# Narrow transposed scores, squares in PSUM, and 2 KB and 16 KB runs for the parts of queries and keys

## The reference

```python
qkv = x @ qkv_w + qkv_b; q, k, v = split(qkv)       # 16 heads of 16
# local attention, blocks of 128 queries; keys from 127 before the block to its end
dist = q_pos - k_pos; allowed = (dist > 0) & (dist <= 128) & (k_pos >= 0)
attn = softmax(where(allowed, q @ k.T / 4, -1e9)); local = attn @ v
# remote attention: each query against means of 8 tokens, 4 heads, chunks before its own
remote = softmax(masked(rq @ rk.T / 4)) @ rv @ rout_w + rout_b
gate = sigmoid(local @ gl_w + remote @ gr_w)
x = layernorm(x + (gate * local + (1 - gate) * remote) @ out_w + out_b)
# feed-forward with ternary weights, each product on its rms-normalized input
h = gelu(ternary(x / rms(x), w_up)); x = layernorm(x + ternary(h / rms(h), w_down))
```

## Time and profile before

| what | us |
|---|---|
| median of 3 runs (1351.72 to 1356.64) | 1356.45 |
| the profiled execution | 1356.7 |
| its span in the profile | 1354.9 |
| TensorE busy in the span | 1125.0 (83%) |
| VectorE busy | 1026.3 (76%) |
| GpSimd busy | 708.1 (52%) |
| ScalarE busy | 671.9 (50%) |

### The profile page before, as it was taken

How to read it: one execution, slowest core, us unless ns; L and a number is a source line. 1 busy time by engine, 2 the same in 40 slices (tenths; PEclk the granted TensorE clock), 3 DMA queues, 4 the chain that set the end, 5 groups by cost and what they waited for, 6 DMA issues and landing times.

```text
span 1354.9 us, 31716 instructions
## 1 busy us (share of the span) xinstructions
PE 1125.0 (83%) x12704; PEld 690.3 (51%) x12704; DVE 1026.3 (76%) x2048; ACT 671.9 (50%) x1024; POOL 708.1 (52%) x866
## 2 busy tenths in 40 slices
PE   4667989897998989897987989798888989785855
PEld 2334545564655556464654555465555545454433
DVE  7755777878877787888787886888787687876566
ACT  2113455564646546464646555464655545462624
POOL 6413546473644636473654646374563647364643
PEclk9676989899988989899999999899898889997877
DMA  6984190846639192754729093663919275471000
GB/s 167 120 111 64 51 124 21 120 70 97 78 85 106 34 124 53 107 82 84 91 68 122 20 128 62 98 76 84 106 45 114 52 104 79 86 80 34 1 16 16
DMA packets 114482, 107.68 MB, mean 79 GB/s; under 512 B 13312, under 2 KB 113792, under 8 KB 114304
## 3 DMA queue, kind: packets, MB, share of 16 engines
q1 hardware_dynamic: 114336, 105.65, 52.2%
HBM read 71.55 MB, written 34.08 MB: 78 GB/s over the span
## 4 chain that ended last, share of the span: by engine, by line
PE 39%; DMA 21%; DVE 20%; SPq 6%; POOL 5%; issue 5%; ACT 3%; DVEq 0%; POOLq 0%
DMA Ks<-parts_scratch 18%; PE oacc L1372 7%; PE work L1321 7%; PE scores L1354 7%; SPq L446 3%; DMA parts_scratch<-parts 3%; DVE x L1035 3%; PE work L1382 3%; SPq L449 2%; DVE x L1043 2%; PE work L1444 2%; PE work L1203 2%; PE work L1326 2%; POOL parts L573 2%; DVE nmax L977 2%
## 5 line engine op out<-in xcount | busy, mean ns | idle before, releaser
L743 ACT ACTIVATE Pt<-scores 128x1024 f32<-128x1024 f32 (+1 forms) x256 | 231.8, 914 | 157.9 <-PE oacc L1372 94.6
L609 POOL TENSOR_TENSOR h_lo<-hbuf,h_hi 128x512 f16<-128x512 f32 x128 | 175.4, 1372 | 239.6 <-DVE h_hi L1088 239.6
L977 DVE TENSOR_REDUCE nmax<-work 128x3 f32<-128x480 f32 x352 | 217.5, 637 | 68.4 <-PE work L1326 64.1
L581 POOL TENSOR_SCALAR_AFFINE_SELECT Pt<-Pt 128x512 f32<-128x512 f32 x256 | 163.3, 638 | 130.4 <-ACT Pt L743 129.5
L1444 PE MATMUL work<-xnT,wup_t 128*128 128x512 f16 x512 | 151.6, 432 | 32.1 <-DVE xnT L1079 32.1
L1321 PE MATMUL work<-Ks,Qs 98*32 98x160 bf16 x4096 | 139.1, 243 | 39.1 <-DMA Ks<-parts_scratch 21.5
L1354 PE MATMUL scores<-Qs,Ks 100*128 100x256 bf16 (+1 forms) x1024 | 144.1, 267 | 3.1 <-ACT Pt L743 1.8
L1372 PE MATMUL oacc<-Pt,Vp 128*32 128x256 f32 (+1 forms) x2048 | 144.9, 360 | 1.9 <-POOL Pt L585 1.8
L1321 PEld LDWEIGHTS work<-Ks,Qs 98*32 98x32 bf16 x4096 | 77.2, 98 | 102.4 <-issue 40.9
L1093 DVE TENSOR_TENSOR oT<-oT,hsq 128x512 f32<-128x512 f32 x112 | 121.5, 1085 | 10.0 <-ACT hsq L784 10.0
L1228 PE MATMUL scores<-xT,wqk 128*128 128x512 f32 x256 | 116.3, 608 | 13.4 <-ACT xT L678 13.4
(11 more groups left out here) (166 smaller groups left out, 2082.0 us busy)
## 6 DMA issues: line engine op xcount, KB each, us to landing
parts_scratch<-parts SPq DMA_DIRECT2D x48, 512.0 KB, 3.0
Qs<-parts_scratch SPq DMA_DIRECT2D x96, 256.0 KB, 14.7
Ks<-parts_scratch SPq DMA_DIRECT2D x96, 256.0 KB, 16.5
xtok<-L_attn_x SPq DMA_DIRECT2D x16, 512.0 KB, 22.4
xres<-L_attn_x SPq DMA_DIRECT2D x16, 512.0 KB, 21.7
y<-ytok SPq DMA_DIRECT2D x16, 512.0 KB, 3.0
Qs<-L_ffn_w_up SPq DMA_DIRECT2D x1, 1024.0 KB, 7.0
Qs<-L_ffn_w_down SPq DMA_DIRECT2D x1, 1024.0 KB, 8.2
```

Source lines behind the costliest of these rows:

```text
L581: ins = pool.affine_select(out=pt[:, :, 0:P], in_=pt[:, :, 0:P], compare_op=ALU.is_gt, fill=0.0, base=0, pattern=[[0, 4], [1, P]], channel ...
L609: pool.tensor_tensor(h_lo[:, t % NR, :], hbuf[:, t % 2, :], h_hi[:, t % NR, :], ALU.subtract).then_inc(h_lo_ready, 1)
L743: nc.scalar.activation(Pt[:, u % NPT, :, 0:w], scores[:, slot, :, :].rearrange("p k (h q) -> p (k h) q", h=2)[:, :, 0:w], ACT.Exp, scale=S ...
L977: nc.vector.tensor_reduce(nmax[:, :, :].rearrange("p b h -> p (b h)")[:, first:first + n], work[:, slot, 0:n * BAND].rearrange("p (h c) -> ...
```

## The change

1. `scores_T` issues for each head and block of keys four matmuls of 32 keys each instead of one of 128; each moves only the queries that its keys can reach (up to 160), into its own 32 partitions of PSUM. Heads are placed in the stacks in another order (`place_of`).
2. The columns of `wqk` are permuted in the prologue (feature first, then head) by ScalarE from a raw copy that lies in `xres`; the bias is loaded to match in eight loads. With that, DRAM holds each part of queries or keys as 128 rows of 2 KB, and each stack row is one run of 16 KB. `Ks` has one padding of 128 columns in all.
3. `restack` writes the query parts as soon as two chunks are ready, waits, reads the six query stacks, then writes the key parts, waits and reads the six key stacks. The wait for the weighing of the sequence before stands ahead of it all.
4. The square is written over the Gelu's input in PSUM; VectorE adds from there, and the slot is free after the add. `hsq` stays only as room for the ternary weights.
5. GpSimd adds the output bias after the last mask, all four blocks in a row.

```diff
+STACKED = 16 * 2 * len(QPART)
+def place_of(h):
+    return h % (H // 2) * 2 + h // (H // 2)
...
-        Ks = [sb(f"Ks{k}", [P, H, P + S], BF16) for k in range(2)]
+        Ks = [sb(f"Ks{k}", [P, P + H * S], BF16) for k in range(2)]
...
-        parts_dram = nc.dram_tensor("parts_scratch", [3, 2 * D, S], BF16, kind="Internal").ap()
+        parts_dram = nc.dram_tensor("parts_scratch", [3, 2, P, 2 * S], BF16, kind="Internal").ap()
...
-            (wqk[:, :, :], qkv_w[:, 0:2 * D].rearrange("(t p) n -> p t n", p=P)),
+            (wqk_raw, qkv_w[:, 0:2 * D].rearrange("(t p) n -> p t n", p=P)),
...
-            (bqk[:, :], qkv_b[0:2 * D].rearrange("(t p) -> p t", p=P)),
...
+        loads += [(bqk[h:P:H // 2, :], qkv_b[0:2 * D].rearrange("(t h d) -> h d t", t=4, d=HD)[h])
+                  for h in range(H // 2)]
...
             def restack(s):
                 if not s.first:
-                    wait_alone(sp, stacks_in[1 - s.par], (s.half + s.par) * (16 * 2 * len(QPART)))
-                for j in range(3):
-                    wait_alone(sp, (part0, part1, part2)[j], count(s, 4, 3))
-                    sp.dma_start(parts_dram[j].rearrange("(t p) n -> p t n", p=P), parts[:, j, :, :]
-                                 ).then_inc(parts_out, 16)
+                    wait_alone(sp, stacks_in[1 - s.par], (s.half + s.par) * STACKED)
                 if s.known and s.i < 2:
                     wait_alone(sp, q_consts, s.i + 1)
                 else:
                     wait_alone(sp, pv_done, count(s, NU, -NU - 1))
-                wait_alone(sp, parts_out, count(s, 1, 0) * 48)
-                for r in range(len(QPART)):
-                    rows = slice(HD * r, HD * r + HD)
-                    sp.dma_start(Qs[s.par][rows, :, :],
-                                 parts_dram[QPART[r], 0:D].rearrange("(h d) n -> d h n", d=HD)
-                                 ).then_inc(stacks_in[s.par], 16)
-                    sp.dma_start(Ks[s.par][rows, :, P:P + S],
-                                 parts_dram[KPART[r], D:2 * D].rearrange("(h d) n -> d h n", d=HD)
-                                 ).then_inc(stacks_in[s.par], 16)
+                for k in range(2):
+                    for j in range(3):
+                        wait_alone(sp, (part0, part1, part2)[j], count(s, 4, 2 * k + 1))
+                        sp.dma_start(parts_dram[j, k], parts[:, j, 2 * k:2 * k + 2, :].rearrange("p t n -> p (t n)")
+                                     ).then_inc(parts_out, 16)
+                    wait_alone(sp, parts_out, count(s, 2, k) * 48)
+                    for r in range(len(QPART)):
+                        rows = slice(HD * r, HD * r + HD)
+                        stack = Qs[s.par][rows, :, :].rearrange("p h n -> p (h n)") if k == 0 else \
+                            Ks[s.par][rows, P:P + H * S]
+                        sp.dma_start(stack, parts_dram[(QPART, KPART)[k][r], k].rearrange(
+                            "(d h) n -> d (h n)", d=HD)).then_inc(stacks_in[s.par], 16)
...
                     mask(s, u)
...
-                    if u % NB == NB - 1:
-                        add_bias(s, u // NB)
+                for b in range(NB):
+                    add_bias(s, b)
...
+                    gelu = nc.scalar.activation(hbuf[:, t % 2, :], work[:, slot, :], ACT.Gelu)
+                    if t == 0:
+                        gelu.then_inc(w_taken[slot], 1)
+                        act.wait_ge(w_taken[slot], n + 1)
+                    else:
+                        gelu.then_inc(h_act, 1)
+                        act.wait_ge(h_act, count(s, FT - 1, t - 1))
-                    nc.scalar.activation(h_sum[:, :] if t == 0 else hsq[:, t % 2, :], hbuf[:, t % 2, :],
+                    nc.scalar.activation(h_sum[:, :] if t == 0 else work[:, slot, :], hbuf[:, t % 2, :],
                                          ACT.Square).then_inc(h_sq, 1)
...
+            for t in range(KT):
+                nc.scalar.activation(wqk[:, t, :].rearrange("p (c d h) -> p c d h", c=4, d=HD),
+                                     wqk_raw[:, t, :].rearrange("p (c h d) -> p c d h", c=4, d=HD),
+                                     ACT.Copy).then_inc(wqk_ready, 1)
...
-                        nc.vector.tensor_tensor(h_sum[:, :], h_sum[:, :], hsq[:, t % 2, :], ALU.add
-                                                ).then_inc(h_added, 1)
+                        nc.vector.tensor_tensor(h_sum[:, :], h_sum[:, :], work[:, slot, :], ALU.add
+                                                ).then_inc(w_taken[slot], 1)
...
                 for c in range(4):
-                    mm = nc.tensor.matmul(scores[:, slot, c // 2, (c % 2) * 2 * P:(c % 2) * 2 * P + w],
-                                          kk[0:KB, 4 * hg + c, P + j * P:2 * P + j * P],
-                                          q[0:KB, 4 * hg + c, j * P:j * P + w], start=True, stop=True)
+                    place = place_of(4 * hg + c)
+                    key = P + place * S + j * P
+                    for g in range(NG):
+                        lo, hi = g * GT, min(g * GT + BAND, w)
+                        mm = nc.tensor.matmul(
+                            scores[g * GT:(g + 1) * GT, slot, c // 2,
+                                   (c % 2) * 2 * P + lo:(c % 2) * 2 * P + hi],
+                            kk[0:KB, key + lo:key + lo + GT],
+                            q[0:KB, place, j * P + lo:j * P + hi], start=True, stop=True)
```

More of the change, by code:

```diff
@@ L287, in build @@
         ones_set = sem("ones_set")
+        wqk_ready = sem("wqk_ready")
         consts = sem("consts")
@@ L335, in build @@
         xn_hi = sem("xn_hi")
+        h_act = sem("h_act")
         h_sq = sem("h_sq")
@@ L357, in build, with in_blocks @@
         nat = nat_all[:, 0:FT * D], nat_all[:, FT * D:FT * D + KT * F]
-        ternary = [t[:, :, :].rearrange("p k n -> p (k n)").bitcast(BF16) for t in (hbuf, hsq)]
+        ternary = [t[:, :, :].rearrange("p k n -> p (k n)").bitcast(BF16) for t in (hbuf, tern_up)]
         below = Vp[:, 1, :, :].rearrange("p b n -> p (b n)").bitcast(BF16)[:, 0:FT * D]
+        wqk_raw = xres[:, :, :].rearrange("p b d -> p (b d)").rearrange("p (t n) -> p t n", t=KT)
         def in_pairs(stack):
-            return stack[:, :, :].bitcast(F32)
+            flat = stack[:, :, :].rearrange("p h n -> p (h n)") if len(stack.shape) == 3 else stack[:, :]
+            return flat.bitcast(F32)
+        def in_blocks(rows):
+            return rows.rearrange("p (b c) -> p b c", c=P)
         ONE_PAIR = float(np.array([0x3F803F80], np.uint32).view(np.float32)[0])
@@ L420, in load_xres @@
             def load_xres(s):
-                if not s.first:
+                if s.first:
+                    wait_alone(sp, wqk_ready, KT)
+                else:
                     for t in range(2):
@@ L571, in p_step @@
                     if t == 0 and not s.first:
-                        pool.wait_ge(parts_out, count(s, 1, -1) * 48)
+                        pool.wait_ge(parts_out, count(s, 2, -1) * 48)
                     pool.tensor_tensor(parts[:, 2, t, :], qk_rest[:, t % 2, :], parts[:, 1, t, :],
@@ L684, in p_step @@
                     if t == 0 and not s.first:
-                        act.wait_ge(parts_out, count(s, 1, -1) * 48)
+                        act.wait_ge(parts_out, count(s, 2, -1) * 48)
                     nc.scalar.activation(parts[:, 0, t, :], p_bank(bank), ACT.Identity,
@@ L778, in f_step @@
                         act.wait_ge(h_sq, count(s, FT, t - 2))
-                    nc.scalar.activation(hbuf[:, t % 2, :], work[:, slot, :], ACT.Gelu
-                                         ).then_inc(w_taken[slot], 1)
-                    act.wait_ge(w_taken[slot], n + 1)
-                    if t >= 3:
-                        act.wait_ge(h_added, count(s, FT - 1, t - 3))
-                    nc.scalar.activation(h_sum[:, :] if t == 0 else hsq[:, t % 2, :], hbuf[:, t % 2, :],
+                    gelu = nc.scalar.activation(hbuf[:, t % 2, :], work[:, slot, :], ACT.Gelu)
+                    if t == 0:
+                        gelu.then_inc(w_taken[slot], 1)
+                        act.wait_ge(w_taken[slot], n + 1)
+                    else:
+                        gelu.then_inc(h_act, 1)
+                        act.wait_ge(h_act, count(s, FT - 1, t - 1))
+                    nc.scalar.activation(h_sum[:, :] if t == 0 else work[:, slot, :], hbuf[:, t % 2, :],
                                          ACT.Square).then_inc(h_sq, 1)
@@ L1084, in f_step @@
                     slot, n = work_use(s, "F", 6 + t)
-                    dve.wait_ge(w_taken[slot], n + 1)
+                    if t == 0:
+                        dve.wait_ge(w_taken[slot], n + 1)
+                    else:
+                        dve.wait_ge(h_act, count(s, FT - 1, t - 1))
                     if t >= NR:
@@ L1312, in max_scores @@
                 if v == 0:
-                    pe.wait_ge(stacks_in[s.par], (s.half + 1) * (16 * 2 * len(QPART)))
```

(4 more changed lines are left out.)

26 lines of the change are left out of this document (14 added, 12 removed).

## The result

The kernel after takes 1307.53 us (1306.51 to 1308.41, 4 runs), the kernel before beside it 1354.09 (1348.58 to 1356.64, 4 runs): ratio 0.9661, 95% interval 0.9626 to 0.9696. The forecast was 1325, with 1286 to 1357 as its range. The gain is 46.6 us where 32 were expected, and it comes mostly from another part of the change than the one that the forecast paid.

The account below looks back on a forecast made before the run. TensorE's first-half work and the chain from parts through stacks to first maxima were taken as bounds. From 1356.7 us, fifteen first halves give -36, the last sequence -2, the prologue +6: 1325 us, range 1286 to 1357.

Parts of the forecast that it names:

- Narrow scores: First half, TensorE's score matmuls: 0.25 us less for each of 12 groups, 0.10 for each of 4; 3.4 us per sequence.
- 2.5 us saved behind the wait: First half after the wait for stacks: 2.9 us of the score saving lies there, less 0.4; bounds 1.0 and 2.9.
- The 0.4 us for coupling to VectorE: First half: deducted because TensorE's 20.5 us would be near VectorE's 19.4 and maxima pass through two PSUM slots.
- Rival C: First half becomes VectorE's, with two slots: only 1.0 of 2.5 us is kept, 1346 us; chance 0.14.
- the stacks then land at the old time (0.0): Restack: 1.3 us later at the old rate, but an estimated 112 GB/s (28.1 us) makes it 0.0; slow end 2.9 later.
- Q can start earlier: Restack: GpSimd's third part of chunk 1 is ready before that of chunk 3, so Q starts 2.8 us earlier.
- The ports: Stack transfers: 16 adjacent partitions reach 4 of 16 ports, 104 GB/s by the skill; 16 KB runs bring nothing.
- The wait: Between the halves TensorE waits for the last stack transfer, 21.5 us over 12 of 14 restacks; stacks later by 0.0.
- rival A: Stack transfers: longer runs load faster, no wait for stacks is left, 4.8 us per sequence, 1289 us; chance 0.17.
- The clock: TensorE's clock drops after waits: 0.1 us taken off the saving in each of fifteen first halves.
- Prologue: Before the first QK matmul: eight bias loads (4.5 us) and ScalarE's permuting copies (1.5): +6 us, between +4 and +8.
- D: Instruction fetch: 3072 more matmuls and 16 KB runs cost TensorE one 2.4 us turn per sequence, +38, 1363 us; chance 0.06.

Follow-up runs that it names:

- split_longer: The kernel before with the new order of the stacks alone, and 12 score matmuls per sequence issued twice: 1342.39 us, ratio 0.9932.

## Why the prediction was right, and where it was wrong

**Narrow scores.** TensorE's timeline of the kernel after:

```profile
722.11 0.46 PE L1385 MATMUL scores<-Qs,Ks 100*32 100x160 bf16 x16 [0.22 <-ACT Pt L760]
722.39 0.38 PE L1348 MATMUL work<-Ks,Qs 98*32 98x160 bf16 x12
...
723.20 0.39 PE L1385 MATMUL scores<-Qs,Ks 100*32 100x128 bf16 x16
723.63 0.39 PE L1348 MATMUL work<-Ks,Qs 98*32 98x160 bf16 x12
```

The price of twelve of the sixteen units was right: sixteen narrow matmuls take 0.28 us (722.11 to 722.39; 0.29 forecast). That of the four units of the last key block was wrong: 0.43 us (723.20 to 723.63; over the 13 periods the median is 0.42, with some at 0.26), where 0.23 was forecast and the wide ones took 0.33. So most of them cost 0.1 us each and save nothing, and the price of the whole is nearer 12 x 0.26 - 4 x 0.10 = 2.7 us a sequence than 3.4. "2.5 us saved behind the wait", and 0.5 ahead of it, was mis-sized with it: with no wait for stacks and full clock the period gains 1.73 us. The 0.4 us for coupling to VectorE was too little; about 1.0 of 2.7 is gone. Rival C's mechanism, the two slots of the maxima, has some of it: TensorE's wait for the maxima is 21.5 us with the order alone and 27.5 with narrow scores added, 0.4 a sequence. The 1.20 us wait above is its place. The rest is not traced.

**Restack, "the stacks then land at the old time (0.0)".** This is the step that failed: they land 46.6 us after QK instead of 50.7. Two of its terms were off. "Q can start earlier", 2.8: measured 4.0. The parts come the 2.8 earlier as read; the other 1.2 fits the write that SyncE waits for, 256 KB now instead of 512 (with the old order and writes of 256 KB it is 1.1). And the time from the first stack to the last, which my terms put at 34.35 us at 112 GB/s (2.15 + 28.1 + 2.3 + 1.8): with 1 KB runs and just those 112 GB/s it is 32.7, so issue, landing, K's writes and the turn cost 4.6 together and not 6.25, because K's writes run partly beside Q's stacks. Those two, 1.1 in that kernel (its first stack is issued 15.3 us after QK) and 1.65, are the 2.7 us of the order alone. The longer runs take 1.3 more off (31.4).

**The ports.** The Trainium skill's 104 GB/s for 16 partitions ("SBUF — State Buffer", Door 1) was within 3% of the 107 with 1 KB runs. That longer runs bring nothing was the prediction's conclusion from it. The measured 117 over 18 us and 126 over 10 us with 16 KB runs contradict the figure and the conclusion; the measurement decides. It was no reason for the forecast's error, though: order without the rate did the same.

**The wait.** The forecast left it whole; it went, and that is rival A's end by a third way: neither rate nor bytes, but a start 4 us sooner. It was worth 1.6 us per period (2.58 -> 0.97 from the first scores to the maxima in the order alone), 21 of the 32 us that the order brought. The other 11 lie where the clock fell before and did not in the profiled execution of the order alone: 0.75 per period in the feed-forward (19.50 -> 18.75), 0.21 between QK and it.

**The clock**, "0.1 us a sequence", was the term that nobody had. In the kernel after, the 19 added matmuls bring 0.7 us per period back (74.28 -> 73.58), and against their eleven periods without a fall (73.37) it is 0.9.

**Squares** 0: shown in the periods. VectorE's addition 685 ns against the 692 forecast. **Prologue** +6: 6.4 at the first QK matmul, given back before the loop. **Bias** -2 at the end: not shown; put back, the stretch behind the periods is 193.2 us against 193.9. **D**, instruction fetch: TensorE's idle put down to issue at the maxima is 2.0 us after (6.2 before); with narrow scores alone it is 9.8 us, 5.5 of it once, so there is something of it, but far from 2.4 us in each sequence.

That the total came out within the range is partly luck. The forecast paid for the narrow scores, too much of it, and put nothing on the order, which brought most; its wait for the stacks stayed in the sum and was gone in the run. The two errors had opposite signs, and the range was wide enough (1286 to 1357) for what they left, 17.5 us.

## What to carry to other kernels

When a chain is late by 2 to 4 us, ask first what starts it and how much each link waits for, not how fast it runs: splitting one batch of transfers where its first half is ready did as much here as the layout that moves faster, and a wait of 1.6 us can be taken away only once. Look at the granted clock by period, over many periods, and ask of each fall what it costs: falls of the same total length cost nothing or 0.7 us by their place. Where they cost, idle time beside the path has a price, and filling the gaps with matmuls that nobody reads can take it away. And undo each part of a large change by itself; here 2 of 5 edits were enough for all of it.

## What was not expected of the hardware

The same thin place of TensorE (2.6 of 4 us busy) costs the clock in some sequences and in others not: none of 13 in the profiled execution of the order alone, 18 falls with 1.25 us more work in the period. And the mean granted clock says little by itself: executions of the order alone at 0.928 and 0.963 took 1317.0 and 1317.1 us, while in split_longer one long fall cost 0.8 us and two short ones 0.1. A kernel can thus get slower by more than the work that is added to it: 12 matmuls worth 1.25 us a period made the 13 periods 21.8 us longer, where 13 times 1.25 are 16.3. Transfers into 16 partitions moved at 107 to 112 GB/s in runs of 1 KB and at 117 to 126 in windows of 10 to 18 us with runs of 16 KB. Where the 4.2 us behind the last period went stays open.
